# Second attention layer: slots' transposes and value products by pairs, first tile of each batch ranked from its far end

## What is computed

```python
x = x + _L0_attn_ref(_layernorm(x), ...)   # 4 x 512 tokens of 128
x = x + _L0_ffn_ref(_layernorm(x), ...)
x = x + _L1_attn_ref(_layernorm(x), ...)   # touched by the change
x = x + _L1_ffn_ref(_layernorm(x), ...)

# _L1_attn_ref, 16 heads of 64, T = 512
att = jnp.einsum('bhqd,bhkd->bhqk', q, k) * (1.0 / math.sqrt(hd))
att = jnp.where(causal[None, None], att, neg_inf)
S = jnp.maximum(att[:, 0], 0.0)
S = jnp.where(keepS[None], S, 0.0)                 # not column 0, not the diagonal
S_shifted = jnp.roll(S, 1, axis=-2).at[:, 0, :].set(0.0)
FF = jnp.cumsum(S_shifted, axis=-2)
att = att - FF[:, None]
memory_budget = max(1, int(T * 0.2))               # 102
FF_mod = jnp.where(causal[None], FF, jnp.inf)
sorted_idx = jnp.argsort(FF_mod, axis=-1)          # the 101 smallest of a row are kept,
...                                                # and the diagonal
y = jax.nn.softmax(att, axis=-1) @ v
y = y.transpose(0, 2, 1, 3).reshape(B, T, H * hd)
y = y @ W_proj.T + b_proj
```

## Time and profile before

| | us |
|---|---|
| time, median of 3 runs | 1010.16 (1009.35 to 1012.23) |
| span of the profiled execution | 1014.7 |
| TensorE busy | 905.4 |
| VectorE busy | 734.6 |
| ScalarE busy | 643.8 |
| GpSimd busy | 537.6 |

### The profile page before, as it was taken

The page is one execution under the profiler, slowest core; times in us unless marked ns, Lnnn a source line. Parts: engine busy times, 40 slices in busy tenths (PEclk is TensorE's granted clock), DMA queues, the critical chain, the costliest instruction groups (busy, mean ns, idle before and its releaser), DMA issues. The chain is left out here.

```text
span 1014.7 us, 19335 instructions
## 1 busy us (share of the span) xinstructions
PE 905.4 (89%) x6140; PEld 606.1 (60%) x6140; DVE 734.6 (72%) x2087; ACT 643.8 (63%) x1433; POOL 537.6 (53%) x664
## 2 busy tenths in 40 slices
PE   8899989998999999988999999989998988962396
PEld 5444444444678888865556666656665755652296
DVE  5676777763889999877997978697878878444022
ACT  2566656554778888844867677767777767740174
POOL 4234536243703344001668766877777778942344
PEclk9999999986999999999999999999999989985599
DMA  4000001000444433140000000000000000002882
GB/s 137 1 1 1 22 1 44 1 24 10 121 138 127 131 104 111 35 120 1 2 1 2 1 2 1 2 1 2 2 1 2 1 2 1 2 1 67 278 286 95
DMA packets 31130, 47.73 MB, mean 47 GB/s; under 512 B 3804, under 2 KB 18673, under 8 KB 30912
## 3 DMA queue, kind: packets, MB, share of 16 engines
q1 hardware_dynamic: 29104, 43.42, 14.2%
q0 software_dynamic: 1504, 3.17, 0.9%
q10 hardware_dynamic: 432, 0.01, 0.0%
HBM read 40.25 MB, written 6.79 MB: 46 GB/s over the span
## 5 line engine op out<-in xcount | busy, mean ns | idle before, releaser
L1507 POOL TENSOR_SCALAR probs<-probs,rinv 128x128 f32<-128x128 f32 (+3 forms) x256 | 274.7, 1086 | 102.1 <-DVE rinv L1372 102.0
L1442 ACT ACTIVATE probs<-probs,rowmin 128x128 f32<-128x128 f32 (+3 forms) x256 | 141.7, 559 | 30.1 <-DVE rowmin L1366 29.0
L1366 DVE CUSTOM_DVE_ANT_0 probs<-psum,adj 128x128 f32<-128x128 f32 (+3 forms) x256 | 122.2, 478 | 50.0 <-PE psum L1227 49.4
L1451 ACT ACTIVATE pt<-psum 128x128 f32<-128x128 f32 (+3 forms) x256 | 98.4, 435 | 69.1 <-PE psum L1237 66.9
L841 ACT ACTIVATE pT<-psum 128x1024 f32<-128x1024 f32 (+3 forms) x128 | 89.6, 702 | 61.9 <-PE psum L597 60.9
L1227 PE MATMUL psum<-k_sb,q_sb 64*128 64x256 f32 (+3 forms) x512 | 110.5, 484 | 17.5 <-DVE rowmin L1366 17.2
L769 DVE TENSOR_REDUCE top<-psum 128x2 f32<-128x256 f32 (+3 forms) x128 | 102.3, 818 | 19.7 <-PE psum L577 19.5
L1355 DVE MAX8 top<-w 128x8 f32<-128x131 f32 (+3 forms) x208 | 103.1, 496 | 4.6
L1815 ACT ACTIVATE r_hid<-psum,b1t 128x512 f32<-128x512 f32 x125 | 82.8, 689 | 33.0 <-PE psum L1654 28.8
L1237 PEld LDWEIGHTS psum<-ident,probs 128*128 128x128 f32 x640 | 68.4, 142 | 58.3 <-POOL probs L1507 37.6
L1237 PE MATMUL psum<-ident,probs 128*128 128x128 f32 x640 | 99.5, 286 | 0.8 <-POOL probs L1507 0.8
(11 more groups left out here) (306 smaller groups left out, 1914.1 us busy)
## 6 DMA issues: line engine op xcount, KB each, us to landing
r_share<-shares SPq DMA_DIRECT2D x12, 1024.0 KB, 7.1
s_wb<-in_w_all SPq DMA_DIRECT2D x23, 514.5 KB
sorted_x<-blank SPq DMA_DIRECT2D x1, 2967.0 KB, 11.9
s_xg<-sorted_x SPq DMA_DIRECT2D x23, 129.0 KB, 2.8
r_w1s<-in_w SPq DMA_DIRECT2D x16, 128.0 KB, 5.8
r_w2s<-in_w SPq DMA_DIRECT2D x16, 128.0 KB, 6.2
r_share<-shares SPq DMA_DIRECT2D x6, 256.0 KB, 3.4
r_share<-shares SPq DMA_DIRECT2D x2, 768.0 KB, 5.0
```

The source lines that it names most:

```text
L1366: dve.tensor_tensor_reduce(probs[:, k, 0:K], s_bank[h][:, 0:K], adj[:, OFF[i]:OFF[i] + K], 1.0, FLOOR, ALU.add, ALU.min, rowmin[:, k:k + 1 ...
L1442: act.activation(probs[:, k, 0:K], probs[:, k, 0:K], ACT.Exp, bias=rowmin[:, k:k + 1], scale=-1.0, accum_out=rsum[:, k:k + 1]).then_inc(ex ...
L1451: act.activation(pt[:, (2 * n + h) % 4, 0:K], t_bank[h][:, 0:K], ACT.Copy).then_inc(pt_ready, 1)
L1507: pool.tensor_scalar(probs[:, k, 0:K], probs[:, k, 0:K], rinv[:, k:k + 1], None, ALU.mult).then_inc(normed, 1)
```

## The change

TensorE's steps go by pairs of slots. In an even step n: scores of n, then the rs fills of n and n+1, transposes of n-4, the other fills of n and n+1, transposes of n-3. In an odd step n: scores of n, value products of n-5 and of n-4. `fills_at` returns both slots' fills for even n and nothing for odd n. ScalarE empties its fills in the same step, one after the first exp and the rest after the second, in place of the start of the next step; VectorE's place for its own is as it was, at the start of step n+1. TURN_LAG is 4, the x fill, the norm ahead of it and the out fill are moved by one slot or two. Tile 0 of each batch has 128 columns, of which 101 are kept: the 27 farthest are sought in place of the 101 nearest, so its decays are written in reversed order and with the other sign, ranked for 8 steps in place of 26, and GpSimd reads them back reversed. The planner's constants are as they were; it now counts 8 steps for those tiles.

```diff
@@ -27,6 +27,7 @@
 FLOOR = 1e36
 TAKEN = -3e38
 SENTINEL = 1e37
+FARTHEST = 1e38
 NOWHERE = 1 << 30
 
 
@@ -1015,24 +1016,27 @@
             TILES = B * NT
             NS = B * SLOTS1
             KEEP = max(1, int(N * 0.2)) - 1
-            PAD = -KEEP % 8
-            ROUNDS = (KEEP + PAD) // 8
+            SOUGHT = [P - KEEP if i == 0 else KEEP for i in range(NT)]
+            PAD = [-SOUGHT[i] % 8 for i in range(NT)]
+            RANKS = [2 * (SOUGHT[i] + PAD[i]) // 8 for i in range(NT)]
+            RANK_BASE = [t // NT * sum(RANKS) + sum(RANKS[0:t % NT]) for t in range(TILES + 1)]
             PR = 12
-            TURN_LAG = 3
+            TURN_LAG = 4
             PV_LAG = 4
-            WOFF = [OFF[i] + PAD * i for i in range(NT)]
+            WOFF = [OFF[i] + sum(PAD[0:i]) for i in range(NT)]
             SCALE = -1.0 / math.sqrt(D1)
             wo = attn_weights[1][3]
 
 
             V_LATE = (0, 1, 2, 3, 4, 5)
-            X_AT = 7
+            X_AT = 6
+            NORM_AT = 3
             Q_AT = (8, 10, 11, 13, 15, 17, 19, 21)
             K_AT = (9, 10, 12, 14, 16, 18, 20, 22)
             RS_AT = (12, 13, 14, 15)
             DEC_AT = (18, 19, 20, 26)
             V_EARLY = (30, 31)
-            OUT_AFTER = 13
+            OUT_AFTER = 14
             RANK_EARLY = 3
             PENALTY_AT = 3
             RANK_COST = (0.33, 0.46, 0.6, 0.73)
@@ -1040,6 +1044,10 @@
             BY_DVE = ("rs", "dec", "out", "bv")
 
             def fills_at(n):
+                both = [] if n % 2 else fills_of(n) + fills_of(n + 1)
+                return [u for u in both if u[0] == "rs"] + [u for u in both if u[0] != "rs"]
+
+            def fills_of(n):
                 b, l = divmod(n, SLOTS1)
                 out = []
                 if n >= OUT_AFTER and (n - OUT_AFTER) % PAIRS == 0 and (n - OUT_AFTER) // PAIRS < TILES:
@@ -1056,14 +1064,14 @@
                 elif l in V_LATE:
                     out.append(("v", b, 2 + V_LATE.index(l)))
                 if b + 1 < B:
+                    if l in RS_AT:
+                        out.insert(0, ("rs", b + 1, RS_AT.index(l)))
                     if l == X_AT:
                         out.append(("x", b + 1, 0))
                     if l in Q_AT:
                         out.append(("q", b + 1, Q_AT.index(l)))
                     if l in K_AT:
                         out.append(("k", b + 1, K_AT.index(l)))
-                    if l in RS_AT:
-                        out.append(("rs", b + 1, RS_AT.index(l)))
                     if l in DEC_AT:
                         out.append(("dec", b + 1, DEC_AT.index(l)))
                     if l in V_EARLY:
@@ -1110,8 +1118,8 @@
                 yt = sbt("yt", [P, 2, PAIRS, P])
                 adj = sbt("adj", [P, TOT])
                 rl = sbt("relu", [P, TOT])
-                w0 = sbt("w0", [P, TOT + PAD * NT])
-                w1 = sbt("w1", [P, TOT + PAD * NT])
+                w0 = sbt("w0", [P, TOT + sum(PAD)])
+                w1 = sbt("w1", [P, TOT + sum(PAD)])
                 top = sbt("top", [P, NT, 8])
 
                 s_bank = banks[0:2]
@@ -1265,12 +1273,20 @@
                     for n in range(NSTEP):
                         if n < NS:
                             pe_score(pe, n)
-                        if TURN_LAG <= n < NS + TURN_LAG:
-                            pe_turn(pe, n - TURN_LAG)
-                        if PV_LAG <= n < NS + PV_LAG:
+                        if n % 2 == 0:
+                            for use in fills_at(n):
+                                if use[0] == "rs":
+                                    pe_fill(pe, use)
+                            if TURN_LAG <= n < NS + TURN_LAG:
+                                pe_turn(pe, n - TURN_LAG)
+                            for use in fills_at(n):
+                                if use[0] != "rs":
+                                    pe_fill(pe, use)
+                            if TURN_LAG <= n < NS + TURN_LAG:
+                                pe_turn(pe, n + 1 - TURN_LAG)
+                        elif PV_LAG < n < NS + PV_LAG:
+                            pe_pv(pe, n - 1 - PV_LAG)
                             pe_pv(pe, n - PV_LAG)
-                        for use in fills_at(n):
-                            pe_fill(pe, use)
 
                 def dve_stats(dve, c, tiles):
                     for i in tiles:
@@ -1317,37 +1333,40 @@
                         K = P * (j + 1)
                         if b:
                             dve.wait_ge(adj_ready, (b - 1) * NT + j + 1)
-                        ins = dve.scalar_tensor_tensor(out=w0[:, WOFF[j]:WOFF[j] + K], in0=bank[:, 0:K], scalar=-1.0,
-                                                       in1=causal[:, N - K:N], op0=ALU.mult, op1=ALU.add)
+                        dst = w0[:, WOFF[j]:WOFF[j] + K]
+                        if j == 0:
+                            ins = dve.scalar_tensor_tensor(out=dst[:, ::-1], in0=bank[:, 0:K], scalar=1.0,
+                                                           in1=causal[:, N - K:N], op0=ALU.mult, op1=ALU.subtract)
+                        else:
+                            ins = dve.scalar_tensor_tensor(out=dst, in0=bank[:, 0:K], scalar=-1.0,
+                                                           in1=causal[:, N - K:N], op0=ALU.mult, op1=ALU.add)
                     else:
                         t = b
                         dve.wait_ge(x_biased, t // NT + 1)
                         ins = dve.tensor_tensor(x_tok[:, t, :], x_tok[:, t, :], bank[:, 0:P], ALU.add)
                     ins.then_inc(f_dve, 1)
 
-                PER_TILE = 2 * ROUNDS
-
-
+                RANK_STEPS = [(t, k) for t in range(1, TILES) for k in range(RANKS[t % NT])]
                 RANKED_BY = [0] * NSTEP
-                k = (TILES - 1) * PER_TILE
+                k = len(RANK_STEPS)
                 for n in range(NS - 1, -1, -1):
                     RANKED_BY[n] = k
                     room = RANK_ROOM[n // PAIRS % NT] * (1.3 if n < SLOTS1 - PAIRS else 1.0)
-                    while k and n <= (1 + (k - 1) // PER_TILE) * PAIRS - 1 - RANK_EARLY and room > 0:
+                    while k and n <= RANK_STEPS[k - 1][0] * PAIRS - 1 - RANK_EARLY and room > 0:
                         k -= 1
-                        room -= RANK_COST[(1 + k // PER_TILE) % NT]
+                        room -= RANK_COST[RANK_STEPS[k][0] % NT]
 
                 def dve_rank(dve, t, k):
                     b, i = divmod(t, NT)
                     r, take = divmod(k, 2)
-                    cols = slice(WOFF[i], WOFF[i] + P * (i + 1) + PAD)
+                    cols = slice(WOFF[i], WOFF[i] + P * (i + 1) + PAD[i])
                     src = w0 if r == 0 else w1
                     if k == 0:
                         dve.wait_ge(f_dve, dve_no["dec", b, i])
                         if b:
                             dve.wait_ge(adj_ready, (b - 1) * NT + i + 1)
                     else:
-                        dve.wait_ge(ranked, t * PER_TILE + k)
+                        dve.wait_ge(ranked, RANK_BASE[t] + k)
                     if take:
                         dve.match_replace(out=w1[:, cols], in_to_replace=top[:, i, :], in_values=src[:, cols],
                                           imm_value=TAKEN).then_inc(ranked, 1)
@@ -1374,7 +1393,7 @@
                 def dve_program(dve):
                     for i in range(NT):
                         K = WOFF[i] + P * (i + 1)
-                        dve.memset(w0[:, K:K + PAD], SENTINEL).then_inc(preset, 1)
+                        dve.memset(w0[:, K:K + PAD[i]], FARTHEST if i == 0 else SENTINEL).then_inc(preset, 1)
                     dve.wait_ge(preset, NT)
                     c = Steps(0, 2 * T + 2)
                     dve_stats(dve, c, range(NT))
@@ -1391,7 +1410,7 @@
                             dve_drain(dve, use)
 
                             for k in {("dec", 0, 0): range(3), ("rs", 0, 2): range(3, 6),
-                                      ("rs", 0, 3): range(6, PER_TILE)}.get(use, ()):
+                                      ("rs", 0, 3): range(6, RANKS[0])}.get(use, ()):
                                 dve_rank(dve, 0, k)
                     done = 0
                     for n in range(NSTEP + 1):
@@ -1406,11 +1425,11 @@
                             dve_invert(dve, n - 1)
                         if n < NS:
                             dve_bias(dve, n, 1)
-                        if n % SLOTS1 == X_AT - 2 and n // SLOTS1 + 1 < B:
+                        if n % SLOTS1 == NORM_AT and n // SLOTS1 + 1 < B:
                             dve_norm(dve, n // SLOTS1 + 1)
                         if n < NS:
                             for k in range(done, RANKED_BY[n]):
-                                dve_rank(dve, 1 + k // PER_TILE, k % PER_TILE)
+                                dve_rank(dve, *RANK_STEPS[k])
                             done = RANKED_BY[n]
 
                 def act_root(act, part, t):
```

(29 more changed lines are left out.)

## The result

The changed kernel takes 1044.0 us (median of 4 runs, 1036.9 to 1046.0) beside 1011.1 for the kernel before (4 runs): ratio 1.031, 95% interval 1.026 to 1.036. It is slower, as forecast, but by 33 us where 10 were forecast, and 13 us beyond the end of the range. The profiled execution is the quickest of the four: span 1035.0. Stretches inside the layer repeat to within 0.1 us from batch to batch and from kernel to kernel as long as TensorE's clock does not fall in them, so the readings go by those; a fall makes a stretch 1.2 to 1.6 us longer (slots 12 to 15 of e_pairs, 18.8 us in its second batch with a fall and 17.2 in its third without).

What follows compares the result with a forecast made beforehand. TensorE and VectorE were taken to bound the kernel in turn. First batch +6.9, batches 2 and 3 +5.3, last -2.2 gave +10.0 us: 1020.2 from a median of 1010.16, range 993 to 1031.

Steps and rivals of the forecast that it cites:

- Bound, forms, ranking: Second attention layer: TensorE and VectorE bound in turn; a form change costs 0.15 to 0.17 us; far-end ranking saves VectorE 6.1.
- Rival 3: Joining blocks saves nothing, TensorE's stretches keep their times and the chains grow 3 us a batch: 1031 us, chance 0.07.
- Ranking in slots 24 to 27: Steady batch: with tile 0's ranking shortened, slots 24 to 27 take 12.4 us against 15.06, -2.7.
- The chains of a steady batch: Fills wait for VectorE's emptying behind ranking: slots 12 to 15 +2.8 us, 18 and 19 +1.8, 28 to 31 +2.7.
- its three terms: Steady batch, slots 0 to 7, against 2.6 saved: 0.65 later transposes, 1.0 copy behind a late exp, 1.2 VectorE's lag.
- slots 8 to 11, +0.1 for -0.6: Steady batch, slots 8 to 11: VectorE's work alone sets the time, 9.8 us against 10.40, -0.6.
- +6.9: First batch, entry included: 1.4 us earlier, slots 0 to 7 lose 2.4, later slots -0.6 + 4.4, +2.0 and +0.1.
- four fills in a step behind four ranking steps lose 2.4 in slots 0 to 7: First batch, slots 0 to 7: paired fills wait for emptyings behind four ranking steps, a loss of 2.4 us.
- +5.9: First batch, slots 8 to 31: slots 8 to 15 -0.6 + 4.4 us, 16 to 23 +2.0, 24 to 31 +0.1.
- 0.3 us in one stretch alone: Steady batch, slots 20 to 23: a third fill behind ScalarE's emptying gives back 0.3 us of 0.7 + 0.5 saved.
- Rival 2: New waits halve TensorE's clock once in each of four batches, doubling 2.5 us of chain: +10, 1030 us, chance 0.12.
- After that nothing is saved: Last batch: -2.2 us up to tile 15's ranking, then GpSimd's 12 slots of norms set the end, no further gain.

Runs made afterwards that it cites:

- e_pairs: The changed kernel without the far-end ranking of tile 0, so the pairs alone: 1050.7 us, ratio 1.037 to the kernel before.
- e_rank: The kernel before with only the far-end ranking of tile 0 added, no pairs: 1003.4 us, ratio 0.992 to the kernel before.
- e_last: The changed kernel with the dec and out fills of a pair put behind its other fills: 1033.1 us, ratio 1.018 to the kernel before.
- e_warm3: The changed kernel with filler matmuls ahead of nine waiting fills of the first batch, each within its wait: 1040.1 us, ratio 1.028 to the kernel before.
- e_late: e_last with rs fills also behind the second transposes and out fills two slots later: 1028.3 us, ratio 1.014 to the kernel before.
- e_late_act: e_late with ScalarE emptying all fills of a step before that step's exps: 1004.6 us, ratio 0.994 to the kernel before.
- e_act: The changed kernel with ScalarE emptying all fills of a step before that step's exps: 1052.1 us, ratio 1.038 to the kernel before.
- e_rs_first: The changed kernel with VectorE emptying rs right behind the slot's biases, ahead of its ranking: 1038.1 us, ratio 1.024 to the kernel before.
- e_vv: e_rank with only the value products of two slots joined in pairs: 1005.4 us, ratio 0.994 to the kernel before.
- e_unpair: The changed kernel with each slot's fills back in that slot's own step: 1016.6 us, ratio 1.002 to the kernel before.
- the three kernels e_late_act: e_late_act (1004.6 us) and two variants of it with the output projection in slots 4, 12, 20, 28 (1007.9) or 6, 14, 22, 30 (1008.1).

## Why the forecast was right in sign and too small

**Bound, forms, ranking: right.** The entry is 1.4 us shorter. The end of the second batch in TensorE's timeline, and the page's group of the transposes' weight loads (answer to the earlier trace rows):

```profile
702.76 0.50 PE L1196 MATMUL psum<-wv_hi,xb_hi 128*128 128x512 f32 x1 [2.53 <-DVE x_tok L1346]
...
703.57 1.04 PE L1245 MATMUL psum<-ident,probs 128*128 128x128 f32 x8
704.53 1.13 PE L1235 MATMUL psum<-k_sb,q_sb 64*128 64x512 f32 x4
705.59 1.97 PE L1261 MATMUL psum<-pt,v_sb 128*64 128x128 f32 x32
707.49 0.49 PE L1235 MATMUL psum<-k_sb,q_sb 64*128 64x128 f32 x4
...
L1245 PEld LDWEIGHTS psum<-ident,probs 128*128 128x128 f32 x640 | 73.4, 144 | 46.6 <-POOL probs L1529 24.3
```

Two slots' value products of 512 columns take 1.90 us where two blocks apart take 2.04; the v fill followed by transposes takes 0.81 for 0.90, and the eight transposes behind it 0.96 for 1.03. Rival 3 is out: transposes behind a full-row fill pay nothing extra, though their loads still take 144 ns each, 1.15 us for eight. That speaks again against the rule of the Trainium skill (TensorE: Matmul & The Clock Gate, Part 3, The mechanism), by which a load hides behind matmuls only in another row group. Ranking in slots 24 to 27: 13.2 where I had 12.4 and TensorE's own sum is 12.6; e_rank isolates the gain.

**The chains of a steady batch: right in place and price, with one link missing.** Slots 12 to 15 17.2 (forecast 16.6), 18 and 19 9.05 (8.7), 28 to 31 20.2 (19.9), 0 to 7 +0.2 (+0.2; its three terms were not looked at one by one). The link is ScalarE's emptying, which lies under VectorE's and would keep most of the time without it: e_last takes VectorE out of slots 18 and 19 and 28 to 31 and gets back 0.45 and 1.3 us of the 2.1 and 2.95 lost there. Two small terms were over-hopeful: slots 8 to 11, +0.1 for -0.6, where a q fill waits 0.78 us for ScalarE's emptying, and 24 to 27, -1.9 for -2.7. That is 1.5 of the 2.4 us missed in each; the three chains are 1.1, and the rest nearly cancels. The forecast's adding had two slips of a tenth (3 x 2.5 + 2.2 is 9.7, and the terms of a steady batch add up to +2.55), which change nothing.

**The first batch: the step that failed.** "+6.9" for it (entry included) should have been +20.4. Three terms of it were mis-sized. (1) "four fills in a step behind four ranking steps lose 2.4 in slots 0 to 7": six fills and ten ranking steps stand in slot 0, the same ten that the timeline of before has there (469.44 to 474.28), and behind the emptying come k and a dec of 2.3 us before the next scores, so VectorE, the bound of those slots, is idle for 4.85 us at once; without the clock the term is +4.6. (2) In slots 8 to 31 I had +5.9 and it is +10.3 in e_warm3: slots 18 and 19 alone grow by 3.2 (one fall of the clock still in it), where in the changed kernel a q fill waits 2.30 us for k_sb (1.50 in a steady batch). That wait is for ScalarE's emptying behind an exp. I had priced such a wait of a fill at 0.3 us in one stretch alone; in the first batch of the changed kernel they add up to 7.6 us, and in e_late, where nothing else holds a fill, to 11.1, of which e_late_act leaves 0.2 and is 9.6 us shorter there, clock included. (3) The clock, which the sum had at nothing: +7.0. So the step that failed is the price of the first batch's waits: the length of the queue ahead of the first emptying, ScalarE's emptying beside VectorE's, and the clock's fall behind them.

**Rival 2 came true beside the forecast.** I had given it the point from which it decides (a fall inside batches 0 to 2) and 4 x 2.5 us, and made it an alternative to the forecast. It is a consequence of it: with filler in the waits four of the five falls are gone. That it "never did" so before spoke of a kernel without those waits. In batches 2 and 3 the profile of the changed kernel has no fall, that of e_warm3 has one: slots 12 to 15 take 18.6 us in the second batch with it and 17.2 in the third without, 1.4 for one fall. e_pairs, e_last, e_late, e_act and e_rs_first have one to three falls in these two batches; before, e_rank, e_vv, e_unpair and the three kernels e_late_act have none. The Trainium skill (TensorE: Matmul & The Clock Gate, Part 1, What's actually happening) has the clock fall with idleness; the five windows agree.

**The last batch.** The mask of tile 15 came 1.8 us earlier, counted from the batch's first score, near the 2.2. "After that nothing is saved" missed that something is lost: the last norm of GpSimd is followed by T T, V V and the projection in pairs, and the layer ends 7.15 us after it where it was 6.06:

```profile
923.87 0.15 POOL L2321 IOTA s_ids<- 128x16 int32 x1 [7.15 <-POOLq L1556]
```

What stays open: 3 us of the 33 between the medians, beyond the layer's 30, and how often the clock falls. The changed kernel has one profile, of its quickest run; the mean granted clock is 0.944 in it and 0.934 to 0.940 in the other three runs, and no trace shows where those lost it. Nor does any run explain why the first score comes up to 12 us earlier or later.

## What to carry to other kernels

When fills of two steps are put together, count for each fill which engine empties its bank, and what that in-order engine has ahead of the emptying: the gain is a fraction of a microsecond for each joined block (0.34 a pair here), the loss is a ranking or an exp for each bank that comes round a second time within the step. Emptyings go ahead of long work that nobody waits for soon, such as a ranking (e_rs_first); fills whose emptying is late go last, and the other engine's emptyings ahead of its exps (e_late_act). With the last two mended the pairing is merely worth nothing (0.994 beside 0.992 for e_rank). Take out one wait and look again: here ScalarE's lay under VectorE's. A forecast that adds waits to a busy TensorE has the clock in its sum, not among its rivals, and the length of a queue of ranking is read in the first batch too, not in a steady one alone.

## What the runs showed of the hardware

The granted clock did not follow the waits strictly. It fell at 465.6 behind a wait of 2.06 us; in slots 12 to 15 of the second batch, with waits of 1.79 and 1.04, it stayed at 1.00, and in the same stretch of e_warm3, with the same work, it fell. A stretch at half clock costs less than half of its length, 7.0 us for 20 us; part of it lies under a wait, and VectorE's work is as long as before (20.7 us in slots 0 to 7 of both). Filler matmuls of 0.12 us each kept the clock up but for one stretch of 3.4 us, and where they fitted the wait they cost the chain nothing: from the last matmul of the q fill to the first of the k fill behind the wait, slot 0 takes 2.46 us with them and 2.45 without.
